# Moving the last stage's input loads from SyncE's queue to ScalarE's

## The reference

```
x = x + conv(gn(x), w_re, w_im, bias)     # spectral convolution: rfft2, 32 x 17 modes kept, 4 heads of 16 channels, irfft2
x = x + whiten(gn(x))                     # whitening along the last axis in 16 groups of 16 columns
```

## Time and profile before

| | |
|---|---|
| median of 3 runs | 4003.51 us (3999.24 to 4007.67) |
| the profiled execution, its own time | 3994.17 us |
| its span in the profile | 3992.2 us |
| last stage, in the span | about 2304 to 3992 us |
| busy share of the span | PE 87%, DVE 75%, POOL 49%, ACT 32% |
| DMA, whole span | 251 GB/s, 1001.88 MB |

### The profile page before, as it was taken

How to read it: one execution, slowest core, us unless ns; L and a number is a source line. 1 busy time by engine, 2 the same in 40 slices (tenths; PEclk the granted TensorE clock), 3 DMA queues, 4 the chain that set the end, 5 groups by cost and what they waited for, 6 DMA issues and landing times.

```text
span 3992.2 us, 103563 instructions
## 1 busy us (share of the span) xinstructions
PE 3455.2 (87%) x36101; PEld 2189.4 (55%) x36101; DVE 2986.1 (75%) x4558; ACT 1263.7 (32%) x3240; POOL 1954.9 (49%) x1434
## 2 busy tenths in 40 slices
PE   6999999999999999944256489999999999999997
PEld 5777777777777777633122244444444544444443
DVE  4666666666666666643655579999999999999998
ACT  2333333333333333322100034444444444444442
POOL 2333333333333333410345346666666666666665
PEclk8999999999999999955589899999999999999998
DMA  9777777777777777666189679999999999999998
GB/s 221 222 211 209 218 214 211 222 214 211 216 214 213 216 216 214 180 90 87 17 266 355 221 268 323 323 326 324 324 325 324 321 326 322 323 322 325 323 326 258
DMA packets 626151, 1001.88 MB, mean 251 GB/s; under 512 B 99616, under 2 KB 460080, under 8 KB 626096
## 3 DMA queue, kind: packets, MB, share of 16 engines
q1 hardware_dynamic: 524720, 912.69, 75.4%
q10 hardware_dynamic: 101376, 88.39, 6.5%
HBM read 639.66 MB, written 361.28 MB: 251 GB/s over the span
## 4 chain that ended last, share of the span: by engine, by line
issue 33%; PE 26%; DMA 14%; POOL 13%; ACTq 5%; DVE 4%; ACT 3%; SPq 1%; POOLq 1%; DVEq 0%
PE bank L432 14%; POOL reg L828 12%; DMA gram_d<-gram 9%; DMA reg<-xh_d 5%; ACTq L671 4%; PE bank L442 4%; PE bank L450 2%; ACT gram L663 2%; PE bank L528 1%; PE bank L466 1%; POOL reg L819 1%; PE bank L552 1%; SPq L298 1%; PE bank L474 1%; DVE reg L1003 1%
## 5 line engine op out<-in xcount | busy, mean ns | idle before, releaser
L828 POOL TENSOR_TENSOR reg<-reg,xht 128x1024 f32<-128x1024 f32 (+1 forms) x512 | 1035.1, 2043 | 581.3 <-DVE reg L1115 581.3
L663 ACT ACTIVATE reg<-bank 128x512 f32<-128x512 f32 (+5 forms) x1696 | 817.6, 535 | 1137.5 <-PE bank L603 850.4
L778 POOL TENSOR_TENSOR reg<-reg 128x512 f32<-128x512 f32 x512 | 651.9, 1273 | 1036.2 <-PE bank L442 1000.5
L432 PE MATMUL bank<-reg 128*128 128x128 f32 x8192 | 1028.8, 279 | 31.4 <-DMA reg<-in_x_dram 31.4
L432 PEld LDWEIGHTS bank<-reg 128*128 128x128 f32 x8192 | 962.2, 193 | 82.3 <-issue 82.3
L1121 DVE TENSOR_TENSOR reg<-reg,xht 128x512 f32<-128x512 f32 x256 | 730.6, 2854 | 26.6
L879 DVE COPY xht<-bank 128x256 f32<-128x256 f32 x512 | 217.1, 424 | 587.5 <-PE bank L450 587.5
L1115 DVE STREAM_TRANSPOSE reg<-bank 128x512 f32<-128x512 f32 x1024 | 639.6, 679 | 20.4 <-PE bank L629 16.5
L595 PEld LDWEIGHTS bank<-tab,reg 128*128 128x128 f32 x4096 | 444.9, 140 | 215.8 <-ACT reg L663 207.9
L866 DVE TENSOR_TENSOR reg<-reg 128x512 f32<-128x512 f32 x512 | 505.9, 988 | 56.9 <-DMA reg<-in_x_dram 31.3
L663 ACT ACTIVATE xh<-bank 128x256 f32<-128x256 f32 x512 | 196.0, 383 | 1033.9 <-PE bank L442 807.2
(11 more groups left out here) (125 smaller groups left out, 1876.6 us busy)
## 6 DMA issues: line engine op xcount, KB each, us to landing
reg<-in_x_dram SPq DMA_DIRECT2D x512, 1024.0 KB, 8.5
out_dram<-reg SPq DMA_DIRECT2D x512, 512.0 KB, 8.1
xh_d<-xh ACTq DMA_DIRECT2D x128, 512.0 KB, 6.8
reg<-xh_d SPq DMA_DIRECT2D x128, 512.0 KB, 5.9
gram_d<-gram ACTq DMA_DIRECT2D x64, 256.0 KB, 6.4
reg<-gram_d SPq DMA_DIRECT2D x64, 256.0 KB, 4.8
spec_d<-psu ACTq DMA_DIRECT2D x512, 8.5 KB, 1.9
reg<-in_L_conv_weight_re_dram SPq DMA_DIRECT2D x32, 136.0 KB, 8.1
```

Source lines behind the costliest of these rows:

```text
L432: ins = mm(bank[q // 2 % 2][:, at:at + P], blk, blk, start=c == 0 and t == 0 and half == 0, stop=c == 1 and t == 1, skip_group_check=True)
L663: copy = lambda o, i, **k: nc.scalar.activation(o, i, ACT.Copy, **k)
L778: nc.gpsimd.tensor_tensor(out=halves[:, q % 2, 1], in0=x_in[:, 2 * q:2 * q + 2, 0], in1=x_in[:, 2 * q:2 * q + 2, 1], op=ALU.subtract).then ...
L828: nc.gpsimd.tensor_tensor(out=rows[:, :, cols], in0=rows[:, :, cols], in1=kap[:, e, cols].unsqueeze(1).to_broadcast([P, rows.shape[1], P]) ...
```

## The change

`load` leaves SP's program and enters ACT's. ACT issues the four loads of iteration 0 after it has copied `mwhit` and before its first `v_keep`. In each step it issues the load for the same buffer of the next iteration after the four evictions of the step, behind a wait for `x_re_used` of the step itself. SP is left with the waits and DMAs of the stores, and with nothing between them. Which bytes are moved, their sizes, the buffers and the semaphores stay.

```diff
@@ sync
-            sp.wait_ge(*nth("ms_ready", 1))
-            def load(p, j):
-                sp.dma_start(x_re[:, j], x_q[:, ds(p * 2, 2)]).then_inc(S[f"x_re_in{j}"], 16)
-
...
-            def loads_stores(t, stores=True):
-                for j in range(4):
-                    sp.wait_ge(*nth("x_re_used", t * 4 + j - 3))
-                    load(t * 4 + j, j)
-                    if stores and j % 2 == 0:
-                        store(t * 2 + j // 2 - 4, j // 2)
-
-            for j in range(4):
-                load(j, j)
-            loads_stores(1, stores=False)
-            with sp.Fori(2, NP // 8) as t:
-                loads_stores(t)
+            with sp.Fori(0, NP // 8 - 2) as t:
+                for e in range(2):
+                    store(t * 2 + e, e)
@@ scalar
+            def load(t, j):
+                act.dma_start(x_re[:, j], x_q[:, ds(t * 8 + 2 * j, 2)]).then_inc(S[f"x_re_in{j}"], 16)
+
...
+                    if not last:
+                        act.wait_ge(*nth("x_re_used", t * 4 + j + 1))
+                        load(t + 1, j)
+
+            for j in range(4):
+                load(0, j)
             v_keep(0, 0)
```

## The result

| | before | after |
|---|---|---|
| median | 4003.31 us (7 runs, 3996.94 to 4007.67) | 4033.80 us (7 runs, 4012.09 to 4051.85) |
| ratio | | 1.0075, 95% interval 1.0046 to 1.0103 |
| profiled execution: time, span | 3994.17, 3992.2 us | 4012.09, 4010.3 us |

The change makes the kernel slower by three quarters of a per cent, and its runs spread nearly four times as far (39.8 us from lowest to highest, where it was 10.7).

The account below looks back on a forecast made before the run. DVE was taken as the bound, 98% busy, with DMA near full. Span 3992.2 + 2.8 (start) + 57 (late stores) - 2.8 = 4049, 4051 as time, 4060 us against the median; range 3998 to 4118 for 8 in 10.

Parts of the forecast that it names:

- A quicker supply of x gives nothing; SP's part frees nothing.: Last stage: no steady-part wait for x, and SP idle before each store's issue, so saving 0.
- ACT's issue is hidden.: ACT, each step: one load issue of at most 2.3 us fits its 2.91 or 3.75 us wait; cost 0.
- The rival in which ACT is held up: ACT's load issue waits for SP's four store issues, 0.9 us a half, 107 us, giving 4110 us; chance 0.05.
- The start, 2.8 us.: Start of last stage: first four loads stand behind the copy of `mwhit`, so PE's first transposes begin 2.8 us later.
- The store lands late because loads get in beside it.: Last stage, two queues: store lands after 14.5 us, 0.9 us late; 4012 to 4118 us, chance 0.48.
- 32 s + n x 0.159: Store's packet time before 1.4 us extra: s per store packet, taken 0.26 us; n load packets between, about 30.
- 0.46 us a half, 57 us.: Steady part: each half pays half of the store's 0.9 us lateness; over 124 halves, 57 us.
- 13.57 us: Last stage: time a store has from its first issue to its last landing before DVE needs the buffer.
- 0.93 us of lateness: Last stage: the store's forecast landing of 14.5 us, put 0.9 us late.
- One for one between the queues.: DMA engines alternate between loaded queues, about one packet each, from first-stage counts of 79 and 90 in the same us.
- Loads land in 4 to 8 us.: Sign expected in the changed profile: last-stage loads land in 4 to 8 us instead of 11.
- rival "hidden": With s under 0.23 the store lands within its time and DVE never waits: 4000 to 4008 us; chance 0.36.

Follow-up runs that it names:

- the second: The changed kernel run and profiled once more with no edit: 4025.5 us, ratio 1.0085.
- wide stores: Each store DMA reads 128 partitions, output in another order: on the changed kernel 3987.4 us, ratio 0.9986; on the kernel before 3984.1 us, 0.9974.

## Why the prediction was right

Forecast slower, 4060 us in a range of 3998 to 4118; measured 4033.8. By its steps:

- *A quicker supply of x gives nothing; SP's part frees nothing.* Right: SP's issues became shorter in the median, and a store was still issued 0.26 us behind the end of POOL's shift (3009.92 behind 3005.61 + 4.05; before, 3012.00 behind 3011.75).
- *ACT's issue is hidden.* Right: 0.38 us each time, and halving the loads with all issues in place removes the loss. The rival in which ACT is held up is refuted.
- *The start, 2.8 us.* Mechanism right, size short: 3.7 us. ACT issued the loads as the copy of `mwhit` began and not at its end, so the first `turn` came 2.2 us later against that copy, less than I had put. It then took 1.1 us longer, with the granted clock at 0.50 from 2314.77 to 2318.44 us (before, 0.75 from 2309.60 to 2312.20), which was not in my sum.
- *The store lands late because loads get in beside it.* Right, and shown from both sides: one queue with equally late loads, or half the loads, brings the time back. The forecast landing was 14.5 us; measured 13.4 and 13.5. The mis-sized term is 32 s + n x 0.159, 13.1 us as I put it. Measured packets are s = 0.200 and a load at 0.195: I gave stores a tenth more than their mean and loads their time alone; in truth the sum of the two stayed as it was. The count n was 30, as I had taken it, but by luck: I had let the store start at once and all 30 come from later loads. 21 were loads issued ahead of it, which go first in one queue too; only 10 came through the second queue.
- *0.46 us a half, 57 us.* Too high, and wrong in one step: a late landing is not shared by two halves. Every half has its own store, and a half that begins late issues the next store late as well, so each half pays its lateness in full. The traces say so: beyond 13.57 us the 120 landings add up to 12.4 us in the first profile and 29.8 in the second, and DVE's waits, the short ones included, to 13.1 and 28.8. At full price my 0.93 us of lateness would have cost 115 us and the forecast would have been 4118, the end of the range. So that 4060 came near is in part luck: a landing put 1.1 us too late and a price put at half work against each other. The median store just makes its 13.57 us; DVE waited for the late ones, 39 of the 120 in the first profile and 53 in the second. The waits for PE at its lower clock were not in my sum.
- *One for one between the queues.* Wrong as an average: the rows of the first stage held for one us. In the changed kernel the queues go through in stretches of some 250 packets, mostly one queue at a time, and a shift of the loads by a few us either way lets 25 or 26 packets pass instead of 10.
- *Loads land in 4 to 8 us.* Wrong: 10.3, since they too wait their turn.

The rival "hidden" fell by little: the median store still had 0.1 to 0.2 us of margin, and of the sign that I had set for it, a landing under 13.5 us without waits of DVE, the landing came in and only the waits did not. The Trainium skill (DMA: Bandwidth & Descriptors, "Issuing engines are not separate DMA queues") says that issuing from several engines only saves issue time. That fits the sum of the packets, 0.395 and 0.396 us, but not the time of the kernel, because one kind of transfer had a deadline and the other had none.

**Open.** Which queue a DMA engine takes next the runs don't settle: the counts say how many loads pass a store at each place, not why 10 of a load issued 4.7 us behind it do and 26 of those issued from 3.9 us on. Nor do they tell whether wide stores are quicker by their partitions alone, or what brings PE's clock down behind one late store and not behind another.

## What to carry to other kernels

A single queue is also an order: here it kept work with slack (a load needed 20 us later) from going ahead of work with a deadline (a store that must free its buffer in 13.6 us). Before you give a stream its own queue, look for the transfer with the smallest margin and count what will now run beside it; total bandwidth didn't show it (0.395 us for a pair of packets, against 0.396). The one split that cost nothing here was of the transfers with the deadline, each half from other partitions.

## What the runs showed that I had not expected

- A wait of 2.6 us on DVE left PE idle for 3.32 us, and the granted clock of the next 10 us had a mean of 0.55: one late store cost 2.6 us and then 3.0 us again. In another run PE stood idle 2.75 us and the clock stayed at 1.00.
- With loads in a second queue, moving them 3 us earlier or 4 to 5 us later took the ratio from 1.0085 to 1.0348 and 1.0432. The same late issue in one queue cost nothing (0.9996).
- A store packet of 4 KB took 0.314 us alone, 0.200 us among loads, and 0.161 us when its DMA read 128 partitions.
